# Products of the identity on TensorE in the wait for the first stacks and in step 0 of a transformer block

## The reference

```
c_proj = silu(c) @ W_mod + b_mod                  # six parts: shift, scale, gate, twice
x_norm = modulate(_ln(x), shift_a, scale_a)
q, k, v = split(x_norm @ W_qkv + b_qkv)
x = x + gate_a * (softmax(q k^T * scale) v @ W_proj + b_proj)
q_c = _ln(x) @ W_qc + b_qc;  k_c, v_c = split(_ln(context) @ W_kvc + b_kvc)
x = x + softmax(q_c k_c^T * scale) v_c @ W_cproj + b_cproj
h = gelu(modulate(_ln(x), shift_m, scale_m) @ W_mlp1 + b_mlp1)
x = x + gate_m * (h @ W_mlp2 + b_mlp2)
```

## Time and profile before

| | us |
|---|---|
| median of 3 runs | 878.57 |
| lowest and highest | 877.36, 882.67 |
| the profiled execution | 881.05 |
| its span | 879.1 |
| TensorE busy | 821.4 (93%) |
| VectorE busy | 622.8 (71%) |
| ScalarE busy | 489.7 (56%) |
| GpSimd busy | 406.5 (46%) |

### The profile page before, as it was taken

How to read it: one execution, slowest core, us unless ns; L and a number is a source line. 1 busy time by engine, 2 the same in 40 slices (tenths; PEclk the granted TensorE clock), 3 DMA queues, 4 the chain that set the end, 5 groups by cost and what they waited for, 6 DMA issues and landing times.

```text
span 879.1 us, 19160 instructions
## 1 busy us (share of the span) xinstructions
PE 821.4 (93%) x6960; PEld 621.8 (71%) x6960; DVE 622.8 (71%) x1354; ACT 489.7 (56%) x922; POOL 406.5 (46%) x464
## 2 busy tenths in 40 slices
PE   1697899999999999999999999999999999998977
PEld 1465766777777787877777777778777777675746
DVE  3547689787887878686878788787878687855320
ACT  1233355756657575756575665757565657674431
POOL 1834333637364553636463636446363634241312
PEclk9958689999999999999999999999999999999799
DMA  7442444433434333344334353434434332211101
GB/s 246 159 139 88 127 128 132 115 124 111 124 102 129 110 107 126 110 143 109 119 116 120 116 128 92 131 103 118 129 110 137 106 110 85 63 37 60 25 1 37
DMA packets 93606, 96.10 MB, mean 109 GB/s; under 512 B 18313, under 2 KB 79882, under 8 KB 93130
## 3 DMA queue, kind: packets, MB, share of 16 engines
q1 hardware_dynamic: 93226, 94.34, 35.2%
q10 hardware_dynamic: 288, 0.54, 0.2%
HBM read 39.60 MB, written 4.33 MB: 50 GB/s over the span
## 4 chain that ended last, share of the span: by engine, by line
PE 88%; DVE 4%; issue 2%; DMA 2%; POOL 2%; ACT 1%; SPq 1%; POOLq 0%; DVEq 0%; ACTq 0%
PE bank L735 23%; PE scan L824 15%; PE pv L781 15%; PE bank L768 13%; PE bank L759 7%; PE score L834 6%; PE bank L748 6%; PE bank L714 2%; DVE MX_y L1111 1%; DVE MX_x L1111 1%; SPq L440 1%; DMA d_st_x<-ST_x 1%; ACT P L951 1%; POOL xn_y L591 1%; DVE PT L1026 0%
## 5 line engine op out<-in xcount | busy, mean ns | idle before, releaser
L951 ACT ACTIVATE P<-score 128x512 f32<-128x512 f32 x512 | 283.5, 597 | 218.3 <-PE score L834 213.8
L1111 DVE TENSOR_REDUCE MX_x<-scan 128x2 fp32r<-128x512 f32 x256 | 170.4, 679 | 73.7 <-PE scan L824 73.6
L1111 DVE TENSOR_REDUCE MX_y<-scan 128x2 fp32r<-128x512 f32 x256 | 165.4, 678 | 29.0 <-PE scan L824 27.6
L735 PE MATMUL bank<-xT_y,W 128*128 128x256 f32 x960 | 131.0, 292 | 1.1 <-DVE xT_y L1009 1.1
L768 PE MATMUL bank<-w_down,HH 128*128 128x256 f32 x512 | 127.4, 394 | 1.0 <-ACT HH L914 1.0
L735 PEld LDWEIGHTS bank<-xT_y,W 128*128 128x128 f32 x960 | 122.1, 197 | 6.8 <-issue 2.8
L824 PE MATMUL scan<-KS_x,QS_x 63*128 63x256 f32 x512 | 109.7, 330 | 9.2 <-DVE MX_x L1111 4.8
L824 PEld LDWEIGHTS scan<-KS_x,QS_x 63*128 63x128 f32 x512 | 72.3, 196 | 49.5 <-issue 26.6
L834 PE MATMUL score<-QS_y,KS_y 64*128 64x256 f32 x512 | 105.8, 319 | 1.5 <-ACT P L951 1.4
L768 PEld LDWEIGHTS bank<-w_down,HH 128*128 128x128 f32 x512 | 94.1, 193 | 18.3 <-ACT HH L914 1.2
L824 PEld LDWEIGHTS scan<-KS_y,QS_y 63*128 63x128 f32 x512 | 68.9, 189 | 47.1 <-DVE MX_y L1111 22.6
(11 more groups left out here) (115 smaller groups left out, 1248.0 us busy)
## 6 DMA issues: line engine op xcount, KB each, us to landing
KS_x<-SK SPq DMA_DIRECT2D x96, 128.0 KB, 2.1
QS_x<-SQ_x SPq DMA_DIRECT2D x96, 128.0 KB, 2.1
KS_y<-SK SPq DMA_DIRECT2D x96, 128.0 KB, 2.1
QS_y<-SQ_y SPq DMA_DIRECT2D x96, 128.0 KB, 2.1
x_in<-in_x SPq DMA_DIRECT2D x16, 256.0 KB, 3.2
tn_x<-in_xT SPq DMA_DIRECT2D x16, 256.0 KB, 4.0
c_in<-in_ctx SPq DMA_DIRECT2D x16, 256.0 KB, 4.2
tn_c<-in_ctxT SPq DMA_DIRECT2D x16, 256.0 KB, 3.8
```

Source lines behind the costliest of these rows:

```text
L735: last = nc.tensor.matmul(to[:, i * N:(i + 1) * N], w[p][:, c, (blk + i) * 128:(blk + i + 1) * 128], xT[k][:, q, c, :], start=(n == 0), st ...
L951: nc.scalar.activation(P[:, s % 8, :, :].rearrange("p a n -> p (a n)"), score_bank[s % 2][:, :], ACT.Exp, scale=SCALE).then_inc(s_exp, 1)
L1111: nc.vector.tensor_reduce(MX[s1][:, half, col:col + NB], scan_bank[n % NSCAN][:, :].rearrange("p (a n) -> p a n", a=NB), AXIS.X, ALU.max, ...
```

## The change

A function `keep_busy(to, n)` multiplies the identity by itself n times into the first 128 columns of a bank; nothing reads the results. It is called with n = 20 on the third projection bank at the end of step -1, behind the gates, and with n = 1 on the first score bank in section A of step 0, behind the scans of each slot for which the table has no task (slots 0, 2, 4, 5, 6, 7, 9, 12, 14, 15: ten). TensorE's wait for `s_rowsC` moves from behind section A of step 0 to ahead of it.

```diff
+            def keep_busy(to, n):
+
+                for _ in range(n):
+                    nc.tensor.matmul(to[:, 0:128], ident[:, :], ident[:, :], start=True, stop=True)
+
@@ section, behind the scans and scores of slot s @@
+                    if letter == "A" and t == 0 and all(at != s for _, _, at in tasks_of(PE_PLAN, letter, t)):
+                        keep_busy(score_bank[0], 1)
+
                 run(PE_PLAN, letter, t, slot, tasks)
@@ the loop over the steps @@
             for t in range(FIRST, LAST + 1):
+                if t == 0:
+                    pe.wait_ge(s_rowsC, 1)
                 section("A", t, "x", t, "y", t - 2)
                 if t == 0:
-                    pe.wait_ge(s_rowsC, 1)
                     pe.wait_ge(s_last_x0, 16)
@@ the end of step -1 @@
                     modulation(1, score_bank[1], (2, 3, 4, 5), raw_m2)
                     gates()
+                    keep_busy(bank[NBANK - 1], 20)
```

## The result

| | before | changed |
|---|---|---|
| median of 13 runs, us | 880.88 | 884.16 |
| lowest and highest, us | 870.67, 884.84 | 881.34, 888.14 |
| profiled execution, us | 881.05 | 888.14 |
| its span, us | 879.1 | 886.2 |

The ratio is 1.0053, with a 95% interval of 1.0028 to 1.0077: slower by 0.5%, where 0.4% faster was forecast (875.0 against 878.57). It is inside one per cent, but outside the range of 870.5 to 881.5.

What follows compares the result with a forecast made beforehand. TensorE at half clock was taken to bound section A of step 0. Overhang +2.3, section A -8.3 + 3.0, section B -0.6 gave -3.6 us: 878.57 to 875.0 us, range 870.5 to 881.5 for 8 in 10.

Steps and rivals of the forecast that it cites:

- The clock: Sign to check: TensorE's clock at 1.00 from 31 to beyond 55 us, through section A of step 0.
- Rivals 2 and 3: Clock falls mid section A, 880.1 us, chance 0.17; identity products don't hold the clock from 40.5 us, 886.8 us, 0.08.
- Term 1: Wait behind the gates: 20 products, 40 records at 0.148 us, take 5.9 us and delay section A by 2.3 us.
- Term 2: Wait for s_rowsC moved ahead of section A: already satisfied when TensorE gets there, cost zero.
- Term 3: Section A of step 0 at full clock with ten added products: 12.4 us, ending at 55.0 instead of 57.97.
- the overhang: Part of the 20 products that sticks out of the 3.65 us wait ahead of section A: +2.3 us.
- Of the 3.0 us about 1 us lies in waits: Section A: about 1 us of the ten products' 3.0 us falls in existing waits for VectorE; not subtracted.
- Term 4: Section B of step 0: eight slots take 4.7 instead of 5.35 us, 0.6 gained; step 1 begins 3.6 us earlier.
- No term stands against it behind that.: Behind the start of step 1: nothing counters the 3.6 us gain; the start's weight transfers and memsets are neither moved nor lengthened.

Runs made afterwards that it cites:

- burst_only: The changed kernel without the ten products behind the slots of section A, keeping the 20 in the wait; ratio 1.0019 to the kernel before.
- v_early: The kernel before with v_xa and v_xb moved from section A of step 0 into the wait behind the gates; ratio 1.0006.
- after2: The changed kernel run and profiled again, nothing altered; ratio 1.0061 to the kernel before.
- pad30: The kernel before with 30 small identity products, 120 instructions, in TensorE's idle time ahead of step -1; ratio 1.0041.
- pairs: The changed kernel with seven instead of ten products in section A, none between neighbouring slots of scans that could overlap; ratio 1.0040 to the kernel before.
- pad64: The kernel before with 64 small identity products, 256 instructions, in TensorE's idle time ahead of step -1; ratio 1.0014.

## Why the prediction was wrong

**The clock.** Right: 1.00 from 31 to beyond 58 us, with TensorE busy throughout; it fell at 61.4, behind a stretch of scores alone (58.1 to 61.3: 2.32 of 3.20 us busy). Rivals 2 and 3 did not happen. The rule that the Trainium skill states for transposes ("TensorE: Matmul & The Clock Gate", Part 4) does not reach plain products with the identity: here TensorE did nothing else for 4.6 us and the clock stayed at 1.00.

**Term 1, the burst.** The mechanism was right, the price too high: 4.66 us for 40 records in the chain, 0.1165 each, the lower end of the range that I gave (0.116), not 0.148. Sixteen columns and 128 cost the same here (0.116 and 0.1165). The first scan came at 41.59 instead of 42.6.

**Term 2, the moved wait.** Right: zero.

**Term 3, section A.** This is the term of the sum that failed: it should have made the section 5.3 us shorter (12.4 instead of 17.7) and made it 1.2 us shorter, which the overhang took back. I took two slots' worth of scans from a place where two slots stand together (0.49 for four) and halved it, and the identity's record from a place where four follow one another. With a product behind each slot both prices are wrong: 16 x 0.43 = 6.9 us instead of 3.9, ten products at 0.42 are 4.2 instead of 3.0, six half projections 5.5 as forecast. Together 16.6 us, measured 16.5 from 41.59 to 58.07; I had 12.4. The price list was right for each form in its own company, and the change alters the company. "Of the 3.0 us about 1 us lies in waits" was moot too: with this spacing VectorE waits for TensorE ahead of every maximum of the section (0.15 to 0.64 us each behind the first).

**Term 4, section B.** Eight slots took 4.77 us (58.14 to 62.91) as forecast (4.7), the pv groups 1.86. The scan of step 1 came at 73.81 instead of 74.70, 0.9 earlier, where I had 3.6. Even that was gone by 82 us, where VectorE's first instruction on x starts at 82.20 before and 82.18 after. Between the two the clock was at half from 71.6 to 81.8 us in the changed kernel, but from 71.2 to 74.6 and 78.0 to 81.4 before. The later swing (at half from 88.3 to 101.9 and from 88.7 to 102.3) is the same in both.

**"No term stands against it behind that."** This step failed as well, and it turned a gain of nothing into a loss: of the 4.8 us, about 3.2 went with the length of the program. I had looked for what the added products delay, not for what their number moves: the code of TensorE comes in 56 loads of 16 KB over the same DMA engines as the stacks, and 120 instructions more shift each load against the work. (That queue 8 carries TensorE's code is read from the counts: 56 loads for 14,360 to 14,480 matmuls and weight loads on TensorE, some 256 each, and 57 loads where 256 or more were added.) In section B of step 15 the last piece of QS_y has half a microsecond of slack (before: issued at 758.3, landed 2.1 us later, scan at 760.92 in the timeline), so 1.8 us of delay of that piece are 1.3 us of delay of the kernel, which is the wait of 1.28.

**The scatter.** The profiled execution before took 881 us; runs of that kernel lie between 870.7 and 886.3. An effect of 3.6 us is within what the clock's swings in steps 0 to 2 and in the tail do from one execution to the next (2.6 us at 147 us alone). A time gained in section A has only partly reached the end in any kernel: 3.3 us earlier in `burst_only` and 1.8 in `v_early` gave ratios of 1.0019 and 1.0006.

## What to carry to other kernels

Price a filler in the company in which it will stand: one full-array product between slots that use half of the rows costs itself and the overlap of its neighbours. Fill a wait with no more than the wait holds: the burst of 20 stuck out of it, that of 14 did not, though neither gave a gain that these runs can show. When instructions are added to the engine that ends last, compare the ends of the program too: a longer instruction stream moves its code loads, and a control that adds the same number of instructions in idle time helps to tell that apart from the change itself. One control isn't enough, since padding shifts the clock and other meetings too; look for the wait in the trace of each.

## What the runs showed of the hardware

- 40 float32 records of 128x128 weights and 128 columns, back to back: 0.1165 us each at full clock; a pair of them between scans: 0.42 us at full clock, 0.72 at half.
- Scans of two neighbouring slots (rows 0 to 62 and 64 to 126), four products of 256 columns: 0.44 us together; the same with a full-array product between them: 0.43 us for each two.
- A code load of 16 KB beside stack transfers: the last of three took 3.9 to 4.1 us to land instead of 2.1 in four executions (changed, `after2`, `pad30`, `pairs`), the load begun 1.1 us behind the issue of that transfer each time; in the other kernels, whose loads lay elsewhere, 27.3 us from section A to section B stayed 27.3. The Trainium skill, "Runtime: NRT & Kernel Launch", Terms, says that instruction memory is refilled in blocks of 16 KiB; the trace agrees, with 0.92 MB in 56 transfers.
- VectorE's PN<-PT,rsum (two inputs in SBUF) takes 0.42 us, and longer where one of GpSimd's TENSOR_TENSOR instructions began ahead of it and still has more than 0.3 us to go: what is left of that one and 0.3 us more. In `pad64` it took 1.77 us with 1.48 left, in the kernel before 1.36 with 1.08 left and 0.94 with 0.66 left, ten times alike within 0.02.
- Before its first record of the clock, at 30 us, the profile shows 1.00, but the modulation's 16 records take 1.86 us at 31 us and, in the same kernel's timeline, at 6 us

```profile
6.14 3.56 PE L686 MATMUL score<-OT,P 128*128 128x16 f32 x16 [6.14 <-DVE OT L1153]
```

twice the time, the price of half clock: the 1.00 ahead of the first record is no measurement.
